# A transformer layer in fp32 on one core: the last two slots of its software pipeline written out by hand

## What is computed

```python
def attn_block(y, Z):                      # y = layernorm(x), Z = ctx (64 rows)
    y = layernorm(y + attention(y, y, y, causal=True)) * g1 + beta1
    y = layernorm(y + attention(y, Z, Z)) * g2 + beta2
    h = relu(y @ w1 + b1)                  # 256 -> 1024
    return layernorm(y + h @ w2 + b2) * g3 + beta3

def fp4(v):                                # blocks of 16 along the last axis
    scale = max(amax(|v|) / 6, 1e-12)
    return grid(|v| / scale) * sign(v) * scale

x1 = x + attn_block(layernorm(x), ctx)
xq = fp4(layernorm(x1))
h  = silu(xq @ fp4(w_gate).T) * (xq @ fp4(w_up).T)     # 256 -> 704
x2 = x1 + fp4(h) @ fp4(w_down).T                       # 704 -> 256
```

## Time and profile before

| | us |
|---|---|
| median of 3 runs | 610.94 |
| lowest, highest | 608.77, 611.94 |
| the profiled execution | 609.96 |
| its span, first to last instruction | 608.0 |
| PE busy | 565.3 (93%) |
| DVE busy | 493.5 (81%) |
| ACT busy | 377.9 (62%) |
| POOL busy | 386.7 (64%) |
| mean granted clock of TensorE | 0.975 |

### The profile page before, as it was taken

How to read it: one execution, slowest core, us unless ns; L and a number is a source line. 1 busy time by engine, 2 the same in 40 slices (tenths; PEclk the granted TensorE clock), 3 DMA queues, 4 the chain that set the end, 5 groups by cost and what they waited for, 6 DMA issues and landing times.

```text
span 608.0 us, 12397 instructions
## 1 busy us (share of the span) xinstructions
PE 565.3 (93%) x4021; PEld 537.1 (88%) x4021; DVE 493.5 (81%) x1211; ACT 377.9 (62%) x781; POOL 386.7 (64%) x466
## 2 busy tenths in 40 slices
PE   4797789999999999999999999999999999999765
PEld 3586679999999999999999999999999999989665
DVE  4969978888888888887988888888888878787762
ACT  3655576666758575766666674867666774746331
POOL 3667656686657667676767666676667665765621
PEclk9978989999999999999999999999999999999897
DMA  7700001010201001010101010010101010000000
GB/s 229 234 2 35 2 2 44 1 54 1 60 2 54 2 19 44 0 52 0 60 0 52 0 44 17 9 43 0 60 2 36 1 36 2 18 2 18 0 19 17
DMA packets 18743, 19.30 MB, mean 32 GB/s; under 512 B 1537, under 2 KB 18193, under 8 KB 18705
## 3 DMA queue, kind: packets, MB, share of 16 engines
q1 hardware_dynamic: 18704, 18.82, 10.1%
HBM read 14.62 MB, written 4.19 MB: 31 GB/s over the span
## 4 chain that ended last, share of the span: by engine, by line
PE 75%; issue 6%; DVE 5%; POOL 5%; ACT 2%; POOLq 0%; DVEq 0%; ACTq 0%
PE R L989 6%; PE R L991 5%; PE R L990 5%; PE O L1041 5%; PE TR L894 5%; PE O L1104 4%; PE R L1059 4%; PE R L1061 4%; PE R L1060 4%; PE O L1106 4%; PE O L1105 4%; PE R L894 3%; PE O L1083 3%; PE O L1085 3%; PE O L1084 3%
## 5 line engine op out<-in xcount | busy, mean ns | idle before, releaser
L989 PE MATMUL R<-gu_hi,xqT_hi 128*128 128x352 f32 x256 | 85.6, 334 | 2.8 <-ACT xqT_hi L659 1.0
L695 ACT ACTIVATE hqT_hi<-R 128x768 fp32r<-128x768 f32 x32 | 26.0, 812 | 98.8 <-PE R L894 98.8
L442 POOL TENSOR_TENSOR rs<-mv,neg_half 128x1 f32<-128x1 f32 (+1 forms) x112 | 68.2, 618 | 25.9 <-DVE mv L1368 24.5
L991 PE MATMUL R<-gu_hi,xqT_lo 128*128 128x352 f32 x256 | 82.5, 322 | 0.0
L990 PE MATMUL R<-gu_lo,xqT_hi 128*128 128x352 f32 x256 | 82.4, 322 | 0.0
L1059 PE MATMUL R<-y2T_hi,w_hi 128*128 128x256 f32 x256 | 76.8, 300 | 2.7 <-DVE y2T_lo L1496 1.3
L1104 PE MATMUL O<-w_hi,hT_hi 128*128 128x256 f32 x256 | 74.4, 291 | 0.0
L448 POOL TENSOR_TENSOR hs<-hh,h_rec 128x704 f32<-128x704 f32 x32 | 44.5, 1391 | 44.4 <-DVE h_rec L1404 44.4
L1061 PE MATMUL R<-y2T_hi,w_lo 128*128 128x256 f32 x256 | 72.6, 284 | 0.0
L1060 PE MATMUL R<-y2T_lo,w_hi 128*128 128x256 f32 x256 | 72.5, 283 | 0.0
L1106 PE MATMUL O<-w_hi,hT_lo 128*128 128x256 f32 x256 | 72.0, 281 | 0.0
(11 more groups left out here) (148 smaller groups left out, 1811.5 us busy)
## 6 DMA issues: line engine op xcount, KB each, us to landing
x_in<-in_x SPq DMA_DIRECT2D x16, 256.0 KB, 2.8
x_res<-in_x SPq DMA_DIRECT2D x16, 256.0 KB, 2.8
out<-x SPq DMA_DIRECT2D x32, 128.0 KB, 2.0
ctx_rows<-in_ctx SPq DMA_DIRECT2D x16, 64.0 KB, 2.5
hT<-in_L_xattn_w SPq DMA_DIRECT2D x1, 1024.0 KB, 7.3
hh<-in_L_xattn_w SPq DMA_DIRECT2D x1, 768.0 KB, 8.7
wd_raw<-in_L_ffn_w_down SPq DMA_DIRECT2D x1, 704.0 KB, 9.3
w_raw<-in_L_ffn_w_gate SPq DMA_DIRECT2D x1, 640.0 KB, 4.5
```

The costliest lines, as they stand in the source:

```text
L989: mm(o, xh, gu_hi[:, c, m, cols], start=(c == 0), stop=False)
L991: last = mm(o, xl, gu_hi[:, c, m, cols], start=False, stop=(c == KC - 1))
```

## The change

The steady slots and the head stay as they are. POOL, ACT, PE and DVE leave the general slots at number 18 (`PAIRS + F`), slot 17 ends early on POOL, ACT and DVE, and a hand-written `tail` follows on each; SP keeps its slots. In the tail, `b` and `h` stand for slot 18 and `g` for slot 17, so `(b, g)` names pair 14's h work and pair 15's x work, `(b, h)` pair 15's h work.

- **x1 of tile t0 on VectorE**: `centred` and `scaled_sum`, two scalar_tensor_tensor steps, take the place of `shift`, `norm`, `gamma3` and `x1_sum`. Tile t1 keeps the four steps.
- **x ahead of h**: pair 15's `x_norm` to `unscale_x` and `turn_xq` of t0 stand ahead of the rest of pair 14's h; PE does `turn_xq(15, t0)`, `down(14, t0)`, `gate_up(15, t0)`, and `down(14, t1)` only after `gate_up(15, t1)`. Pair 14's t1 is transposed into the banks `TR1` and `O1` (`split_turn`), so that gate and up may use `R`.
- **The absolute value of h in SBUF**: for pair 14 t1 and pair 15 t0 `abs_rows` writes `ha` and `rows_lift`, `rows_drop` read it there.
- **Column parts**: pair 15's gate and up are cut 384 + 320 instead of 352 + 352. For its last tile the whole way from the block maximum to the down product goes in these two parts, 9 matmuls each (`part_down`).
- **ScalarE**: the three `warm` steps of the end are left out.

Where PE has nothing to do, it waits; nothing fills those waits.

```diff
@@ slots()
-def slots(eng, slot, start):
+def slots(eng, slot, start, end):
-for n in range(PAIRS - HALVES, PAIRS + Q + 2):
+for n in range(PAIRS - HALVES, end):
+HALF = IC // 2 * P
+PARTS = (slice(0, HALF), slice(HALF, FI))
+PART_BLOCKS = (slice(0, HALF // BLK), slice(HALF // BLK, FB))
+TURNED_PARTS = (slice(0, HALF), slice(HALF, IW))
...
@@ slot() of POOL, ACT and DVE, each at its own place
+    if f and not a:
+        return
...
@@ POOL
+def part_scale(s):
+    pool.wait_ge(part_rec, s + 1)
+    n = part_width(s) // BLK
+    pool.tensor_tensor(blocks(hs[:, 1, PARTS[s]]), blocks(hh[:, 1, PARTS[s]]),
+                       per_block(h_rec[:, 1, PART_BLOCKS[s]], n), ALU.mult).then_inc(part_scaled, 1)
...
+def tail(b, h):
+    g = h - 1
+    power(3, b, g, F, (0,))
+    power(4, b, g, F, (0,))
+    scale_h(b, g, 1)
+    scale_x(b, g, 0)
+    power(3, b, g, F, (1,))
+    unscale_x(b, g, 0)
+    pool.wait_ge(ln_out[3], T * PAIRS - 1)
+    pool.tensor_tensor(z3[:, 1, :], z3[:, 1, :], g3_row[:], ALU.mult).then_inc(y3_set, 1)
+    x1_sum(b, g, 1)
+    power(4, b, g, F, (1,))
+    unscale_h(b, g, 1)
+    scale_x(b, g, 1)
+    unscale_x(b, g, 1)
+    scale_h(b, h, 0)
+    unscale_h(b, h, 0)
+    wait(pool, hq_grid, b, g, Q, T, T)
+    wait(pool, hq_turned, b, g, Q, T, T)
+    part_scale(0)
+    part_scale(1)
+    part_unscale(0)
+    part_unscale(1)
...
@@ ACT
+def abs_rows(b, h, t):
+    wait(act, hq_scaled, b, h, Q, T, t + 1)
+    wait(act, hq_set, b, h, Q + 1, T, t + 1)
+    act.activation(ha[:, t, 0:FI], hs[:, t, 0:FI], ACT.Abs, scale=LIFT).then_inc(hq_abs, 1)
...
+def split_upper(b, h):
+    wait(act, hq_turned, b, h, Q, T, T)
+    for o, cols, done in ((TR[1], TURNED_PARTS[0], first_hi), (O[1], TURNED_PARTS[1], hqT_hi_set)):
+        act.activation(hqT_hi[:, 1, cols], o[:, 0:HALF], ACT.Copy).then_inc(done, 1)
...
+def part_lifted_abs(b, h, s):
+    act.wait_ge(part_scaled, s + 1)
+    if s == 0:
+        wait(act, xqT_lo_set, b, h, Q, T, T)
+    else:
+        wait(act, hqT_lo_set, b, h, Q + 1, T, T)
+        act.wait_ge(first_lo, 1)
+    act.activation(part_abs_bank(s), hs[:, 1, PARTS[s]], ACT.Abs, scale=LIFT).then_inc(part_abs, 1)
...
+def tail(b, h):
+    g = h - 1
+    hT_upper(b, g, 0)
+    abs_x(b, g, 0)
+    abs_rows(b, g, 1)
+    wait(act, ln_rstd[3], b, g, F, T, T)
+    act.wait_ge(ln_shift[3], T * PAIRS - 1)
+    act.activation(z3[:, 1, :], z3[:, 1, :], ACT.Identity, bias=nm[3][:, 1:2],
+                   scale=rs[3][:, 1:2]).then_inc(ln_out[3], 1)
+    xT_upper(b, h, 0)
+    last_silu(b, h, 0, 0)
+    last_silu(b, h, 0, 1)
+    abs_x(b, g, 1)
+    split_upper(b, g)
+    xT_upper(b, h, 1)
+    abs_rows(b, h, 0)
+    last_silu(b, h, 1, 0)
+    last_silu(b, h, 1, 1)
+    part_lifted_abs(b, h, 0)
+    last_upper(b, h)
+    part_lifted_abs(b, h, 1)
+    part_upper(0)
+    part_upper(1)
...
@@ PE
+def split_turn(b, h):
+    wait(pe, hq_set, b, h, Q, T, T)
+    wait(pe, z3_set, b, h, F, T, T)
+    for i in range(IC):
+        o, k = (TR[1], i) if i < IC // 2 else (O[1], i - IC // 2)
+        last = turn(o[:, P * k:P * (k + 1)], hq[:, 1, P * i:P * (i + 1)])
+    last.then_inc(hq_turned, 1)
...
+def part_down(b, h, s):
+    pe.wait_ge(part_hi, s + 1)
+    pe.wait_ge(part_lo, s + 1)
+    wait(pe, x2_set, b, h, Q + 1, T, T)
+    o = O[1][:, 0:D]
+    for i in range(IC // 2 * s, IC // 2 * (s + 1)):
+        hi, lo = hqT_hi[:, 1, P * i:P * (i + 1)], hqT_lo[:, 1, P * i:P * (i + 1)]
+        mm(o, hi, wd_hi[:, i, :], start=(i == 0), stop=False)
+        mm(o, hi, wd_lo[:, i, :], start=False, stop=False)
+        last = mm(o, lo, wd_hi[:, i, :], start=False, stop=(i == IC - 1))
+    if s == 1:
+        last.then_inc(down_done, 1)
...
+def tail(b, h):
+    g = h - 1
+    turn_xq(b, h, 0)
+    down(b, g, 0)
+    last_gate_up(b, h, 0, 0)
+    last_gate_up(b, h, 0, 1)
+    split_turn(b, g)
+    turn_xq(b, h, 1)
+    last_gate_up(b, h, 1, 0)
+    last_gate_up(b, h, 1, 1)
+    pe.wait_ge(first_hi, 1)
+    pe.wait_ge(first_lo, 1)
+    down(b, g, 1)
+    last_turn(b, h)
+    part_turn(b, h, 0)
+    wait(pe, x2_set, b, h, Q + 1, T, 1)
+    down(b, h, 0)
+    part_turn(b, h, 1)
+    part_down(b, h, 0)
+    part_down(b, h, 1)
...
@@ DVE
+def centred(b, h):
+    wait(dve, ln_aggr[3], b, h, F, T, 1)
+    dve.wait_ge(rows3_in, 16 * 2)
+    v.scalar_tensor_tensor(z3[:, 0, :], z3[:, 0, :], mv[3][:, 0, 0:1], g3_row[:],
+                           ALU.subtract, ALU.mult).then_inc(y3_set, 1)
+def scaled_sum(b, h):
+    wait(dve, y3_set, b, h, F, T, 1)
+    wait(dve, ln_rstd[3], b, h, F, T, 1)
+    wait(dve, xb_set, b, h, F, T, 1)
+    v.scalar_tensor_tensor(x1[(h - F) % 2][:, 0, :], z3[:, 0, :], rs[3][:, 0:1], xb[:, 0, :],
+                           ALU.mult, ALU.add).then_inc(x1_set, 1)
+def rows_lift(b, h, t):
+    wait(dve, hq_abs, b, h, Q, T, t + 1)
+    v.scalar_tensor_tensor(hs[:, t, 0:FI], ha[:, t, 0:FI], LIFT_MIN, hs[:, t, 0:FI],
+                           ALU.max, ALU.add).then_inc(hq_lifted, 1)
...
+def part_lift(s):
+    dve.wait_ge(part_abs, s + 1)
+    v.scalar_tensor_tensor(hs[:, 1, PARTS[s]], part_abs_bank(s), LIFT_MIN, hs[:, 1, PARTS[s]],
+                           ALU.max, ALU.add).then_inc(part_lifted, 1)
...
+def tail(b, h):
+    g = h - 1
+    ff_sum(b, g, 0)
+    z3_stats(b, g, 0)
+    aggregate(3, b, g, F, 0)
+    centred(b, g)
+    scaled_sum(b, g)
+    x1_stats(b, g, 0)
+    aggregate(4, b, g, F, 0)
+    h_scale(b, g, 1)
+    h_reciprocal(b, g, 1)
+    x_norm(b, g, 0)
+    x_max(b, g, 0)
+    x_scale(b, g, 0)
+    x_reciprocal(b, g, 0)
+    ff_sum(b, g, 1)
+    z3_stats(b, g, 1)
+    aggregate(3, b, g, F, 1)
+    x_lift(b, g, 0)
+    x_drop(b, g, 0)
+    wait(dve, ln_rstd[3], b, g, F, T, T)
+    v.scalar_tensor_tensor(nm[3][:, 1:2], mv[3][:, 1:2, 0], -1.0, rs[3][:, 1:2],
+                           ALU.mult, ALU.mult).then_inc(ln_shift[3], 1)
+    hT_lower(b, g, 0)
+    xT_lower(b, h, 0)
+    rows_lift(b, g, 1)
+    x1_stats(b, g, 1)
+    aggregate(4, b, g, F, 1)
+    rows_drop(b, g, 1)
+    x_norm(b, g, 1)
+    x_max(b, g, 1)
+    x_scale(b, g, 1)
+    x_reciprocal(b, g, 1)
+    last_product(b, h, 0, 0)
+    last_max(b, h, 0, 0)
+    x_lift(b, g, 1)
+    x_drop(b, g, 1)
+    last_product(b, h, 0, 1)
+    last_max(b, h, 0, 1)
+    last_scale(b, h)
+    xT_lower(b, h, 1)
+    split_lower(b, g)
+    down_add(b, g, 0)
+    rows_lift(b, h, 0)
+    rows_drop(b, h, 0)
+    last_product(b, h, 1, 0)
+    last_max(b, h, 1, 0)
+    part_scale(0)
+    last_product(b, h, 1, 1)
+    last_max(b, h, 1, 1)
+    part_scale(1)
+    down_add(b, g, 1)
+    part_lift(0)
+    part_drop(0)
+    last_lower(b, h)
+    part_lift(1)
+    part_drop(1)
+    part_lower(0)
+    down_add(b, h, 0)
+    part_lower(1)
+    down_add(b, h, 1)
...
@@ end of DVE (POOL, ACT and PE alike)
-slots(dve, slot, HEAD)
+slots(dve, slot, HEAD, PAIRS + F)
+tail(B + 1, 0)
```

116 lines of the change are left out of this document (112 added, 4 removed).

## The result

| | before | changed |
|---|---|---|
| median, us | 609.86 (4 runs) | 602.96 (4 runs) |
| lowest, highest | 608.50, 611.94 | 601.69, 604.55 |
| ratio, 95% interval | | 0.9884 (0.9846 to 0.9922) |
| profiled execution, span | 609.96, 608.0 | 603.46, 601.5 |
| PE, DVE, ACT, POOL busy | 565.3, 493.5, 377.9, 386.7 | 562.5, 496.8, 373.2, 386.5 |

The kernel is 6.9 us faster, 1.2%.

The account below looks back on a forecast made before the run. The end was taken as bound by a chain of small steps handed between engines. Gains of 2.4 and 1.8 summed to 4.2 us, giving 606.7 against the median of 610.94, stated as 606.6, range 603.2 to 610.2.

Parts of the forecast that it names:

- Step 1: Pair 15's t0, x1 in two VectorE steps and x ahead of h: xq 4.1 us earlier, 2.4 us left at hq.
- third rival: Low clock reaches into gate and up of pair 15's t0, 24 matmuls at 0.29: 608.9 us, chance 0.12.
- Step 2: Absolute value of h in SBUF: 0 us, reciprocal to hq stays 5.5; table loads left out 0, at most 1.3.
- Step 3: Pair 15's last tile in two column parts: hq of t0 to last add 11.9 instead of 13.7, 1.8 us.
- sign of a wrong step 3: More than 12.5 us between hq of t0 and the last add would show the column-parts term wrong.
- more comes through: Full clock in one or both down products (1.7 us each), or x_norm not held by POOL: 603.3 us, chance 0.10.
- slower: Empty waits keep the clock low through pair 15's gate and up, 48 matmuls, and last down products: 614.6 us, chance 0.04.
- does not do what it says: Pair 15's x is not earlier in time, gate product starts at 579, only the parts earn: 609.1 us, chance 0.06.

Follow-up runs that it names:

- whole: The changed kernel with its last tile (pair 15's t1) in one piece again, new order and x1 kept: 608.73 us, ratio 0.9990 to the kernel before.
- b_warm: The kernel before with TensorE's waits near the end filled by matmuls whose results are unread: 607.36 us, ratio 0.9975 to the kernel before.
- whole_warm: The changed kernel with its last tile in one piece and TensorE's waits filled by unread matmuls: 605.82 us, ratio 0.9945 to the kernel before.
- warm: The changed kernel with three TensorE waits filled by matmuls whose results are unread: 601.67 us, ratio 0.9876 to the kernel before.

## Why the prediction was wrong, by its steps

From `ff_sum` of t0, in us:

| | forecast | after |
|---|---|---|
| `x_norm` starts, lasts | 3.8, 1.6 | 3.9, 1.5 |
| xq of t0 | 9.2 | 9.3 |
| gate product of t0 starts | 13.8 | 13.6 |
| h reciprocal of t0 done | 20.6 | 20.4 |
| hq of t0 | 26.1 | 26.0 |
| last add ends | 38.0 | 38.7, usually 37.1 |

**Step 1** was right in each mark of t0: xq is 4.1 us earlier, half of that comes through behind `down(14, t0)` at the low clock (0.21 apart as said), and TensorE rests 4.95 us. Not foreseen was the low clock in the first half of t1's gate and up (12 matmuls at 0.32 instead of 0.17); it was the third rival's cost in small, and on t1, behind another wait of TensorE. **Step 2** was right: 5.5 from reciprocal to hq stayed 5.6. The table loads are gone; before, ScalarE had waits of 2.3 us or more behind each of the three, so nothing shows that they cost time.

**Step 3** is the term that was mis-sized; it is the step that failed. It read "From 589.6 that is 11.9 instead of 13.7: **1.8 us**". The 11.9 was fair: 11.1 usually (37.1 - 26.0), though 12.7 in the profile above, which is past the 12.5 that the forecast had named as the sign of a wrong step 3. The 13.7 was not: it is the old distance from t0's hq to the end, and was taken over to the new order as if t1 followed 2.5 earlier as well. In the changed kernel t1's xq is ready at 19.5 and was at 18.2 before. whole shows that distance in the new order: 41.5 - 25.9 = 15.6. So the parts earn 4.4 there and not 1.8, and steps 1 and 2 without them 0.8 and not 2.4. That the sum came near is luck: the two errors cancel in part, 4.2 was the sum, 5.2 the usual tail.

A good part of both errors is the clock. With the waits filled the distance is 11.8 in b_warm, 12.8 in whole_warm and 10.0 in warm, and the two terms are 2.1 and 2.7, nearer to 2.4 and 1.8. The forecast had no low clock in t1's gate and up, where the new order puts it, nor in the last down product of the tile in one piece.

**The clock.** I took `down(15, t0)` at 1.2 GHz. That holds in the profile above (0.21 apart; last add at 38.7) but not in three of four (37.1). The full clock brings 1.6 there, and 0.7 of it is lost against the forecast of 38.0. The place can be seen on VectorE, where pair 14's second `down_add` stands ahead of the lift of t1's first part:

```profile
589.31 0.42 DVE L1657 TENSOR_TENSOR x<-O,w_raw 128x256 f32<-128x256 f32 x1 [0.52 <-PE O L1208]
589.65 0.55 DVE L1910 SCALAR_TENSOR_TENSOR hs<-TR,hs 128x384 f32<-128x384 f32 x1
```

It waited for `down(14, t1)`, which t1's slow gate and up had held up, and the drop behind it ended 30.2 behind `ff_sum` instead of the forecast's 29.4. In warm it waits for nothing, and the same drop ends at 28.5. The rival "more comes through" is what usually happens, for one of the two products. The rival "slower" had an error in its price: before, of the last two down products only the last ran at full clock, `down(15, t0)` did not the earlier trace rows.

**The baseline** is the larger part of the miss. The sum was set against 610.94, the median of three runs; later medians of before are 608.6 to 609.4. Of the 3.6 us between forecast and result 1.7 are this, 1.0 the tail, and about 1 is the open part that no profiled execution shows. I had left some 1 us for the scatter of the median; that was too narrow on the low side. With the baseline right the time would have been inside a range that wide.

The rivals "slower" and "does not do what it says" did not occur, and the low clock reached only the first two of the 24 gate and up matmuls of t0.

## What to carry to other kernels

When a chain at the end is shortened, write down for each tile when it is ready, and look for the second chain just behind the first: before, t1 was 0.9 us behind t0, so a gain of 2.5 on t0 alone could not arrive. A distance measured in the old schedule must not be carried into the new one unless both of its ends move together. And test the parts of a change in both sequences: here the order earns 0.8 or 2.0 and the parts 3.2 or 4.4, by what the other has already done. Where the clock falls in such a tail, test with it held as well: 2.1 and 2.7 are what remains.

## What the runs showed of the hardware

Some steps of VectorE and POOL that work on SBUF hold each other: `x_norm` took 1.51 beside a POOL step against 0.41 alone, `x_lift` 1.14 against 0.46. Not all do: in the kernel before, a block maximum of 704 columns took 0.87 at 590.45 beside POOL's `unscale_h` (590.61, 1.39 long), as it does alone, and the lower part of hqT, which reads PSUM, took 0.95 at 569.10 in the changed kernel beside POOL's step at 569.20. I had not expected that POOL is held as well: its `power`, 128 elements in all, took 1.10 (573.00 in the POOL rows of the changed kernel) instead of 0.55 beside `rows_drop` on VectorE (572.84, 0.85 long).

The Trainium skill (Advanced Engine Details and Errata, VectorE Performance Modes) says that VectorE's second SBUF port is shared with GpSimd, and that GpSimd instructions and two-port VectorE instructions block each other. These rows agree in that some steps are held and others not, and in both directions; which of the steps use two ports no trace shows. The other surprise is the granted clock behind short rests: after the same wait of 1.84 us and the same instructions `down(15, t0)` ran at 1.2 GHz in one execution of the changed kernel and at 2.4 in three.
